# A two-layer ViT tower on one core: the Switch layer's weights made stationary and fetched per tile, its router moved into the hyena tail, its last add made by matmul

## The chip, the cores and the metric

The kernel runs on one core of a Trainium2 chip. TensorE does matmuls into the eight banks of PSUM, VectorE and ScalarE read PSUM and compute elementwise, GpSimd computes elementwise and issues indirect DMAs, SyncE (SP) issues most other DMAs. Every engine runs its own instruction stream; they meet through semaphores. The metric is the time of one execution on the device in microseconds, given as the median of several runs. All data is float32, apart from the operands of the filler matmuls.

## What is computed

Four images of 64x64x3 become 256 tokens each of 192 features, plus one class token: 257 x 4 tokens. Two layers follow. The first has attention and a soft mixture of experts. The second has the hyena operator (a long convolution with gates, an RMS norm and a projection) and a Switch mixture of experts. The change touches the second layer only:

```python
def _L1_attn_ref(inputs, w_in, b_in, w_sf, b_sf, h, norm_w, w_out, b_out):
    # hyena: gates, long convolution, then
    ms = jnp.mean(jnp.square(y), axis=-1, keepdims=True)
    y = y * jax.lax.rsqrt(ms + EPS) * norm_w
    y = jnp.einsum('bld,ed->ble', y, w_out) + b_out
    return y + inputs * SKIP

def _L1_ffn_ref(hidden_states, router_w, wi, wo):     # Switch, 8 experts, 192 -> 768 -> 192
    logits = x @ router_w
    probs = jax.nn.softmax(logits, axis=-1)
    p, e_idx = jnp.max(probs, axis=-1), jnp.argmax(probs, axis=-1)
    # every token goes to one expert, and its result is scaled by p
    h = jax.nn.relu(x @ Wi_e) @ Wo_e
    # returned: the sum over experts of combine * h; each layer is then added to its input
```

## The kernel before

Tokens lie in nine tiles of 128 rows (`NT`): two per image, and one tile `TAIL` with the four class tokens in rows 0, 32, 64 and 96. The residual stream is `k.h` [128, 9, 192]. `build` runs the stages one after another with `run`, which frees the stage's semaphores and puts a barrier of all engines behind each.

**Hyena inputs** (`hyena_inputs`). SP loads weights and constants, the first two band matrices `hy_band` (1540 KB each) and eight spread rows `hy_x_spread`, and as its last act here issues `a["wi"]`, the first-layer weights of all eight Switch experts, 4608 KB, into `k.wi` (L1533).

**Hyena mix** (`hyena_mix`). SP loads five constants, `hy_w_out` (576 KB) among them, into one semaphore `w_in`; TensorE waits for all five before the first convolution. 24 steps m follow, in six groups of four, one band matrix to a group: a row matmul `cls_source` (L1743), a convolution of four matmuls in two column groups (L1755), VectorE's gate (L1846), and a sum matmul `sum_y` (L1765). For each group from the third on SP waits for the convolutions two groups back, loads the band and four `hy_x_spread` rows, and at the end `a["wo"]`, the second-layer weights of all Switch experts. Then `project` (L1802) multiplies by `w_out` with 32-row operands, one row group per image; tile 0 of every image first, tile 1 in two halves because bank 7 (`MS`) still holds the mean squares; VectorE adds into `k.h` (L1857). The class tokens are projected last (L1821).

**Switch** (`stage_switch`). It starts with the layer norm of the nine tiles (`Norm`: `bn_stats` L103, `bn_aggr`, a power on GpSimd L118, subtract and scale L111, transposes L135, copies L145). TensorE makes the router logits with 36 instructions of 8 columns (L2040). VectorE finds the expert of each token; TensorE counts ranks by triangular and ones matmuls (L2048, L2052); VectorE makes from them `dest_rows`, a row of a sorted table in DRAM for each token, and `tile_expert`, the expert of each of its 15 tiles. Every expert's tokens start at a new tile. The table was zeroed by 16 DMAs; nine indirect DMAs on GpSimd scatter the normalised tokens into it (L2019). Between these steps stand filler matmuls (`keep_busy`, L82), queued in TensorE's program order.

The loop runs over 15 tiles, in a ring of three. SP loads a tile of x. TensorE transposes it (L2067, two 96-column halves), ScalarE copies it out (L2124). Layer 1 (L2076): x is stationary, the expert's weights are the moving operand, 2 x 2 matmuls of 384 columns, found by a register read `expert_of`. ScalarE and VectorE apply relu to one half each, TensorE transposes the hidden tile (L2085), both engines copy it out (L2133, L2200), layer 2 (L2094) has six matmuls of 192 columns, VectorE copies (L2205), GpSimd stores to a second table (L2024). TensorE's program order in each turn is: turn x of tile t+1, turn h of t, layer 1 of t+1, layer 2 of t.

After the last store nine indirect gathers fetch the results in token order (L2028), and behind the last of them VectorE does `h += token_y * top_prob` nine times (L2230). A further stage `store` issues eight DMAs to the output.

Of the kernel before, what the change touches and what calls it, by code (L numbers as in the profile page):

```python
# [14 lines left out]
STAGES = 5  # L15

P = 128
# [435 lines left out]


def store(k, out):

    stored = k.sem("out_stored")
    with k.nc.Block() as block:
        @block.sync
        def _(sp):  # L460
            for b in range(B):
                sp.dma_start(out[b, 1:L, :].rearrange("(j p) d -> p j d", p=P),
                             k.h[:, JT * b:JT * (b + 1), :]).then_inc(stored, 16)
                sp.dma_start(out[b, 0:1, :], k.h[QUAD * b:QUAD * b + 1, TAIL, :]).then_inc(stored, 16)
            sp.wait_ge(stored, 16 * 2 * B)

# [1028 lines left out]
def hyena_inputs(k, a, x):  # L1495

    nc, ps = k.nc, k.ps
    with ExitStack() as st:
# [17 lines left out]
        with nc.Block() as block:  # L1516
            @block.sync
            def _(sp):
# [13 lines left out]
                if STAGES >= 5:  # L1532
                    sp.dma_start(k.wi[:, :, :, :], a["wi"]).then_inc(k.s_switch_w, 16)  # L1533
# [123 lines left out]
def hyena_mix(k, a, x):  # L1657
# [6 lines left out]
    with ExitStack() as st:  # L1664
# [26 lines left out]
        with nc.Block() as block:  # L1691
            @block.sync
            def _(sp):
                for dst, n in ((bout[:, :], a["hbout"].broadcast_to([P, D])), (nw[:, :], a["hnw"]),
                               (image[:, :], a["himage"]), (tail[:, :], a["htail"]), (wout[:, :, :], a["hwout"])):
                    sp.dma_start(dst, n).then_inc(w_in, 16)
                for g in range(2, NG):
                    sp.wait_ge(conv, GP_ * (g - 1))
                    x.load_band(sp, a, g)
                    sp.wait_ge(gated, GP_ * (g - 1))  # L1700
                    x.load_x0(sp, g)
                if STAGES >= 5:
                    sp.dma_start(k.wo[:, :, :, :], a["wo"]).then_inc(k.s_switch_w, 16)

            @block.gpsimd
            def _(pool):
# [9 lines left out]

                pool.memset(zero[:, :], 0.0).then_inc(zeroed, 1)
# [16 lines left out]
                pool.tensor_tensor(rms[:, :], mse[:, :], k.half[:, :], ALU.pow).then_inc(rms_r, 1)  # L1734

            @block.tensor
            def _(pe):
# [61 lines left out]
                def project(t, b, c):  # L1799
                    row = slice(QUAD * b, QUAD * (b + 1))  # L1800
                    out = (ps[:, 4 * t + b, 0:D] if (t, b) != (1, 3) else ps[:, MS, 0:D])
                    mm = pe.matmul(out, y[row, c, 1 + t * P:1 + (t + 1) * P], wout[row, c, :],  # L1802
                                   start=c == 0, stop=c == NG - 1)
                    if c == NG - 1 and b % 2 == 1:
                        mm.then_inc(proj, 1)

                pe.wait_ge(gated, PAIRS)
                for c in range(NG):
                    pe.wait_ge(y_r, c + 1)
                    for b in range(B):  # L1810
                        project(0, b, c)
                squares(NG - 1)
                for half in ((0, 1), (2, 3)):
                    if half == (2, 3):
                        pe.wait_ge(mse_r, 2)
                    for c in range(NG):
                        for b in half:
                            project(1, b, c)
                pe.wait_ge(yc_r, NG)
                for c in range(NG):  # L1820
                    mm = pe.matmul(ps[:, MS, D:2 * D], yc[:, c, :], wout[:, c, :], start=c == 0,  # L1821
                                   stop=c == NG - 1)
                mm.then_inc(proj_c, 1)

            @block.scalar
            def _(act):
                act.wait_ge(w_in, 80)
                for c in range(NG):
# [3 lines left out]
                                   ).then_inc(y_r, 1)  # L1832

            @block.vector
            def _(dve):
# [24 lines left out]
                for t in range(JT):  # L1860
                    for b in range(B):
                        if b % 2 == 0:
                            dve.wait_ge(proj, 2 * t + b // 2 + 1)
                        if (t, b) == (1, 3):
                            dve.wait_ge(proj_c, 1)
                            add(TAIL, TAIL, ps[:, MS, D:2 * D])
                            add(JT * b + t, B * t + b, ps[:, MS, 0:D])
                        else:
                            add(JT * b + t, B * t + b, ps[:, 4 * t + b, 0:D])
# [52 lines left out]
HH = HID // 2  # L1922


def alloc_switch(k, a, st):

    k.wi = k.sb("switch_wi", [DK, SE, DC, HID], F32, st)
# [3 lines left out]
    k.sorted_y = k.nc.dram_tensor("sorted_y", ((ST + 1) * P, D), F32, kind="Internal").ap()  # L1931


def stage_switch(k, a):
    nc, ps = k.nc, k.ps
    with ExitStack() as st:
# [3 lines left out]
        rw = sb("router_w", [DK, DC, SE])  # L1940
        tri = sb("before", [P, P])
        desc = sb("descending", [P, NT, SE])
        steps = sb("tile_steps", [P, SE, TOKEN_TILES])
        lower = sb("lower", [P, SE, SE])
        valid = sb("valid", [P, NT])
        spare = sb("spare", [P, NT])
        tile_no = sb("tile_no", [1, ST, SE])
        zeros = sb("zeros", [P, D])
        lm = sb("lm", [P, NT])
        sh = sb("sh", [P, NT, SE])  # L1950
        pe_ = sb("pexp", [P, NT, SE])
        psum_ = sb("prob_sum", [P, NT])
        top = sb("top_prob", [P, NT])
        eq = sb("eq", [P, NT, SE])
        first = sb("first_max", [P, NT])
        oh = sb("one_hot", [P, NT + 1, SE])
# [389 lines left out]
```

## Time and profile before

| | us |
|---|---|
| median of 3 runs | 814.07 |
| lowest and highest | 811.37 and 817.34 |
| the profiled execution | 815.75 |
| its span, first to last instruction | 814.1 |
| mean granted TensorE clock in it | 0.950 |
| TensorE busy | 713.6 (88%) |
| VectorE, ScalarE, GpSimd busy | 287.0, 223.5, 141.5 |

Times in the rows are microseconds from the start of the span. A matmul of float32 appears as two instructions, so "x12" means six matmuls. TensorE's matmuls are listed under PE, its weight loads under PEld, which overlap. The granted clock is given as a share of full speed: 1.00 is 2.4 GHz and 0.50 is 1.2 GHz. In the chain of waits every piece is what the next one waited for.

### The profile page before, as it was taken

To read this page: it belongs to the slowest core of one execution; us is meant where nothing else is said; L and a number is where in the kernel's file an instruction comes from. 1 tells how busy PE (TensorE), PEld (TensorE's weight loads), DVE (VectorE), ACT (ScalarE), POOL (GpSimd) and SP (SyncE) were. 2 spreads that over 40 slices of the span, in tenths; PEclk is the share of its full clock that TensorE was granted. 3 is DMA by queue.
4 is the path that set the end of the run, shared out by engine and by line. 5 is a ranking of instruction groups with operands and counts; after the bars stand their busy time and mean duration, and the time that the engine had idled before them with its cause. 6 is when DMAs were issued, how large, how long until landed. Compare 5 with 4: busy or idle time off the path is not lost. (4 is left out here: it accounts for less than half of the span.)

```text
span 814.1 us, 11798 instructions
## 1 busy us (share of the span) xinstructions
PE 713.6 (88%) x4265; PEld 493.4 (61%) x4266; DVE 287.0 (35%) x618; ACT 223.5 (27%) x486; POOL 141.5 (17%) x194
## 2 busy tenths in 40 slices
PE   4587999999998889899999999989789989699960
PEld 3355854545455444389999998734535655477750
DVE  0003345454552598613233232036312152122211
ACT  2332124333332244244444441014200110122210
POOL 6761201011000053300000000000062113011023
PEclk9998999999999999999999999999679998799995
DMA  8318000000000030038888880035937821111002
GB/s 219 85 8 231 0 2 1 1 1 1 1 2 0 1 78 1 0 98 257 254 261 249 257 249 1 1 122 174 237 91 265 336 88 35 39 39 39 24 24 78
DMA packets 28087, 78.37 MB, mean 96 GB/s; under 512 B 7698, under 2 KB 17934, under 8 KB 26738
## 3 DMA queue, kind: packets, MB, share of 16 engines
q1 hardware_dynamic: 25090, 74.02, 30.7%
q0 software_dynamic: 2960, 3.84, 1.9%
q8 instruction: 26, 0.43, 0.2%
q14 instruction: 11, 0.09, 0.0%
HBM read 72.21 MB, written 5.63 MB: 96 GB/s over the span
## 5 line engine op out<-in xcount | busy, mean ns | idle before, releaser
L1358 PE MATMUL banks<-slots,soft_w 96*128 (+1 forms) x768 | 90.9, 275 | 1.6 <-PEq L1111 1.6
L1358 PEld LDWEIGHTS banks<-slots,soft_w 96*128 96x128 f32 x768 | 89.8, 192 | 1.8 <-issue 1.8
L1418 DVE COPY eo<-banks 32x192 f32 x128 | 45.3, 354 | 106.6 <-PE banks L1369 103.6
L1404 ACT ACTIVATE hid<-banks,soft_b 128x128 f32<-128x128 f32 x192 | 55.5, 368 | 61.4 <-PE banks L1358 61.3
L861 DVE TENSOR_REDUCE nm<-banks 128x2 f32<-128x906 f32 x48 | 53.0, 1103 | 44.2 <-PE banks L661 44.2
L1369 PE MATMUL banks<-soft_w,hid 128*128 128x192 f32 x384 | 67.5, 326 | 0.0
L825 ACT ACTIVATE pt<-banks 128x1024 f32<-128x1024 f32 (+1 forms) x48 | 49.0, 1023 | 58.5 <-PE banks L687 58.5
L1369 PEld LDWEIGHTS banks<-soft_w,hid 128*128 128x128 f32 x384 | 61.7, 190 | 0.0
L661 PE MATMUL banks<-kt,qt 32*128 32x453 f32 x192 | 49.4, 590 | 6.2 <-DVE nm L861 3.8
L82 PE MATMUL banks<-dense 128*128 128x512 bf16 x170 | 44.1, 414 | 11.0 <-PEq L2264 8.7
L687 PE MATMUL banks<-qa,kt 32*128 32x256 f32 (+1 forms) x384 | 51.5, 386 | 0.0
L705 PE MATMUL banks<-pt,vt 128*32 128x257 f32 (+2 forms) x384 | 51.0, 386 | 0.4 <-ACT pt L825 0.3
L2076 PE MATMUL banks<-switch_wi,tile_xt 96*128 x120 | 45.3, 523 | 0.7 <-ACT tile_xt L2124 0.6
L687 PEld LDWEIGHTS banks<-qa,kt 32*128 32x128 f32 (+1 forms) x384 | 32.4, 172 | 12.9 <-issue 9.0
L82 PEld LDWEIGHTS banks<-dense 128*128 128x128 bf16 x170 | 17.1, 105 | 34.0 <-issue 16.2
L1537 POOL MEMSET hy_u<- 96x16 f32 x1 | 0.1, 113 | 201.2 <-POOLq L2264 201.2
L1155 PE MATMUL banks<-phi,xt 96*128 96x512 f32 x72 | 33.8, 618 | 0.0
L705 PEld LDWEIGHTS banks<-pt,vt 128*32 128x32 f32 (+2 forms) x384 | 18.2, 109 | 24.4 <-issue 8.2
L2094 PEld LDWEIGHTS banks<-switch_wo,tile_ht 128*128 128x128 f32 x180 | 30.0, 190 | 4.9 <-issue 1.2
L2094 PE MATMUL banks<-switch_wo,tile_ht 128*128 x180 | 31.8, 326 | 0.9 <-DVE tile_ht L2200 0.9
L2076 PEld LDWEIGHTS banks<-switch_wi,tile_xt 96*128 96x128 f32 x120 | 22.7, 199 | 16.0 <-issue 3.2
L1132 POOL TENSOR_TENSOR cw<-ex,f 128x1024 f32<-128x1024 f32 x9 | 23.2, 2572 | 46.3 <-ACT f L1227 46.3
(267 smaller groups left out, 986.4 us busy)
## 6 DMA issues: line engine op xcount, KB each, us to landing
soft_w<-in_sw SPq DMA_DIRECT2D x64, 576.0 KB, 5.5
hy_band<-in_hband SPq DMA_DIRECT2D x6, 1540.0 KB, 6.6
switch_wi<-in_wi SPq DMA_DIRECT2D x1, 4608.0 KB, 24.9
switch_wo<-in_wo SPq DMA_DIRECT2D x1, 4608.0 KB, 16.3
hy_x_spread<-x_rows SPq DMA_DIRECT2D x24, 128.5 KB, 5.1
vt<-in_vt SPq DMA_DIRECT2D x1, 2496.0 KB
dwc_spread<-dispatch_cls SPq DMA_DIRECT2D x1, 1536.0 KB, 9.0
sorted_x<-zeros SPq DMA_DIRECT2D x16, 96.0 KB, 1.7
```

The costliest lines, as they stand in the source:

```text
L82: pe.matmul(k.ps[:, bank, :], k.dense[:, 0:P], k.dense[:, :], start=True, stop=True)
L661: mm = pe.matmul(ps[:, q, 0:NK], qt[row, c, b, j * P:(j + 1) * P], kt[row, c, b, :], start=True, stop=True)
L687: mm = pe.matmul(ps[0:kr, 2 + s % 2 * 2 + q, u * NP_:(u + 1) * NP_], kt[row, c, b, at:at + kr], qa[row, n % 2, :], start=True, stop=True)
L705: mm = pe.matmul(ps[QUAD * g:QUAD * (g + 1), 6, 0:L], vt[0:vr, tile, at:at + VW], pt[0:vr, s % 4, q, u, :], start=t == 0, stop=t == 3)
L825: act.activation(pt[0:kr, s % 4, :, :, 0:NP_], ps[0:kr, at:at + 2, :].rearrange("p g (t q) -> p g t q", t=2), ACT.Exp).then_inc(exped, 1)
L861: dve.tensor_reduce(nm[:, n % 2, j, at:at + QUAD + 1:QUAD], ps[:, 0:2, 0:NK], AXX, ALU.max, negate=True).then_inc(maxed, 1)
L1358: mm = pe.matmul(ps[:, 2 * (r % 2) + j // 3, (j % 3) * P:(j % 3 + 1) * P], k.w1[r][:, d, j * P:(j + 1) * P], rhs, start=d == 0, stop=d == ...
L1369: mm = pe.matmul(ps[:, 4 + r, 0:D], hid[:, r % 2, j, :], k.w2[r][:, j, :], start=j == 0, stop=j == HJ - 1)
L1404: ins = act.activation(hid[:, r % 2, j, :], ps[:, 2 * (r % 2) + j // 3, (j % 3) * P:(j % 3 + 1) * P], ACT.Gelu, bias=k.b1[:, ds(i * R + r, ...
L1418: dve.tensor_copy(eo[SL * r:SL * (r + 1), b, ds(i, 1), :].rearrange("p e d -> p (e d)"), ps[SL * b:SL * (b + 1), 4 + r, 0:D]).then_inc(eo_ ...
L2076: mm = pe.matmul(ps[:, 1 + c, 0:HH], xst[:, d, :], k.wi[:, ds(e, 1), d, c * HH:(c + 1) * HH].rearrange("p e n -> p (e n)"), start=d == 0, ...
L2094: mm = pe.matmul(ps[:, 5 + r, 0:D], hst[:, j, :], k.wo[:, ds(e, 1), j, :].rearrange("p e n -> p (e n)"), start=j == 0, stop=j == HJ - 1)
```

## The change

It has five parts.

1. `k.wi` and its load in `hyena_inputs` are gone. Each of the 15 tiles loads its expert's first-layer weights, 128 x 1152 floats (576 KB), into a ring of three. SP reads the expert from `tile_expert` into a register and issues the load; it can do so only in the Switch stage.
2. Layer 1 is turned round: the weights are stationary and x moves, 128 columns. K = 192 is split into 128 and 64. The 64-row parts are laid out in the two halves of the partitions, so that even and odd column blocks use different row groups. The product comes out already transposed; `turn_h` and its two copies are gone. The turning of x is one transpose of 128 columns and two matmuls with the identity that write the last 64 features to both halves.
3. Norm, router, zeroing of the tables and scatters move from the Switch stage into the end of the hyena mix (`Route`). The norm is done in two groups, four tiles and five. `project` does tile 1 of all images at once. The zeroing DMAs and router constants are issued by SP near the start of the mix.
4. The router has fewer steps: one comparison fused with a product, the spare rows folded into constants, the totals from a separate small matmul.
5. The last add is made on TensorE: `k.h` by the identity into PSUM, then each gathered tile times a diagonal of `top_prob`, each with a semaphore of its own. ScalarE copies out and SP stores, within the same stage; the stage `store` is gone.

```diff
@@ hyena_inputs, SP
-                if STAGES >= 5:
-                    sp.dma_start(k.wi[:, :, :, :], a["wi"]).then_inc(k.s_switch_w, 16)
@@ hyena_mix, SP, behind the five loads of w_in
+                k.route.load(sp, a)
@@ hyena_mix, GpSimd: first k.route.clear(pool); behind the power of rms:
+                k.route.gpsimd(pool)
@@ hyena_mix, TensorE
+                pe.wait_ge(mse_r, 2)
                 for c in range(NG):
+                    project(1, c)
                 pe.wait_ge(yc_r, NG)
+                pe.wait_ge(h2, 2)
...
                 mm.then_inc(proj_c, 1)
+                k.route.tensor(pe)
@@ hyena_mix, VectorE
+                dve.wait_ge(proj, 1)
+                for b in range(B):
+                    add(JT * b, b, ps[:, b, 0:D])
+                k.route.moments(dve, 0, h2)
+                dve.wait_ge(proj, 2)
+                for b in range(B):
+                    add(JT * b + 1, B + b, ps[:, 4 + b, 0:D])
+                dve.wait_ge(proj_c, 1)
+                add(TAIL, TAIL, ps[:, 1, 0:D])
+                k.route.normalize(dve, 0)
+                k.route.moments(dve, 1, h2)
+                k.route.normalize(dve, 1)
+                k.route.vector(dve)
@@ Route
+    def load(self, sp, a):
+        for dst, n in ((self.rw[:, :, :], "rw"), (self.tri[:, :], "before"), (self.desc[:, :, :], "desc"),
+                       (self.steps[:, :, :], "steps"), (self.lower[:, :, :], "lower"),
+                       (self.tile_no[:, :, :], "tile_no"), (self.place[:, :, :], "place0")):
+            sp.dma_start(dst, a[n]).then_inc(self.c_in, 16)
+        sp.wait_ge(self.zero, 1)
+        for t in range(ST + 1):
+            sp.dma_start(k.sorted_x[t * P:(t + 1) * P, :], self.zeros[:, :]).then_inc(self.cleared, 16)
+        sp.dma_start(k.sorted_y[ST * P:(ST + 1) * P, :], self.zeros[:, :]).then_inc(self.cleared, 16)
+    def tensor(self, pe):
+        keep_busy(k, pe, 0, 8)
+        pe.wait_ge(self.c_in, 112)
+        for n in range(4):
+            turn_x(n)
+        for n in range(4):
+            logits(n)
+        keep_busy(k, pe, 0, 8)
+        for n in range(4, NT):
+            turn_x(n)
+        for n in range(4, NT):
+            logits(n)
+        keep_busy(k, pe, 0, 5)
...
+        mm.then_inc(self.rank, 1)
+        keep_busy(k, pe, 0, ROUTE_FILL)            # ROUTE_FILL = 60
@@ stage_switch, SP
+                def load_wi(i, r):
+                    e = sp.value_load(tei[0:1, ds(i * RING + r, 1)], min_val=0, max_val=SE - 1)
+                    sp.dma_start(wi[r][:, :], a["wi"][ds(e, 1)].rearrange("e p n -> (e p) n")).then_inc(wi_in[r], 16)
+                sp.wait_ge(route.te_r, 1)
+                for r in range(RING):
+                    load_wi(0, r)
+                sp.wait_ge(route.scattered, 16 * NT)
                 for r in range(RING):
                     sp.dma_start(xs[r][:, :], k.sorted_x[r * P:(r + 1) * P, :]).then_inc(xs_in[r], 16)
                 with sp.Fori(1, TURNS) as i:
                     for r in range(RING):
                         sp.wait_ge(xt_m, (i - 1) * RING + r + 1)
                         sp.dma_start(xs[r][:, :], k.sorted_x[ds((i * RING + r) * P, P), :]).then_inc(xs_in[r], 16)
+                        sp.wait_ge(h_m, ((i - 1) * RING + r) * 2 + 2)
+                        load_wi(i, r)
@@ stage_switch, TensorE
                 def turn_x(i, r):
                     pe.wait_ge(xs_in[r], i * 16 + 16)
+                    pe.transpose(ps[:, 0, 0:P], xs[r][:, 0:DA], k.ident[:, :])
+                    for q in range(2):
+                        mm = pe.matmul(ps[q * DB:(q + 1) * DB, 0, P:2 * P], xs[r][:, DA:D], k.ident[:, :],
+                                       start=True, stop=True)
                     mm.then_inc(xt_m, 1)
+                def layer1(i, r, first=False):
+                    pe.wait_ge(wi_in[r], i * 16 + 16)
                     pe.wait_ge(xt_r, i * RING + r + 1)
+                    if not first:
+                        pe.wait_ge(h_a, i * RING + r)
+                        pe.wait_ge(h_v, i * RING + r)
+                    for j in range(HJ):
+                        pe.matmul(ps[:, 1 + j % 2, (j // 2) * P:(j // 2 + 1) * P], wi[r][:, j * P:(j + 1) * P],
+                                  xst[:, 0, :], start=j < 2, stop=False)
+                    for j in range(HJ):
+                        half = slice(j % 2 * DB, (j % 2 + 1) * DB)
+                        mm = pe.matmul(ps[:, 1 + j % 2, (j // 2) * P:(j // 2 + 1) * P],
+                                       wi[r][half, HID + (j // 2) * P:HID + (j // 2 + 1) * P], xst[half, 1, :],
+                                       start=False, stop=j >= HJ - 2)
...
                 with pe.Fori(0, TURNS - 1) as i:
                     for r in range(RING):
                         nxt = (i + (r + 1) // RING, (r + 1) % RING)
                         turn_x(*nxt)
-                        turn_h(i, r)
                         layer1(*nxt)
                         layer2(i, r)
...
+                pe.wait_ge(diag_r, NT)
+                for n in range(NT):
+                    pe.wait_ge(gathered[n], 16)
...
+                    mm = pe.matmul(ps[:, n // 2, at:at + D], diag[:, n, :], yg[:, n, :], start=False, stop=last)
@@ stage_switch, VectorE
-                for t in range(NT):
-                    dve.wait_ge(gathered, 16 * NT)
-                    dve.scalar_tensor_tensor(k.h[:, t, :], yg[:, t, :], top[:, t:t + 1], k.h[:, t, :],
-                                             ALU.mult, ALU.add).then_inc(added, 1)
@@ build
-        run(k, store, out)
```

## Rows read from the trace of the kernel before

**Rows 1.** Chain of waits in the tile loop: start us, us, what.
```profile
698.08 0.65 PE banks L2067 x2
698.75 0.39 ACT tile_xt L2124
...
740.00 2.75 PE banks L2076 x8
742.75 1.95 PE banks L2094 x12
744.70 0.22 PE banks L2067 x2
...
783.68 0.67 PE banks L2085 x6
...
785.28 2.23 PE banks L2094 x12
```

**Rows 2.** Window table: us, busy us (x instructions) per engine, granted clock, DMA share, GB/s.
```profile
600.00:605.00 5.00, 5.00 (x18) 2.44 (x16) 0.85 (x2) 0.00 (x0) 4.92 (x2) 0.50 0.01 3
655.00:659.00 4.00, 2.73 (x20) 2.21 (x16) 2.33 (x7) 0.00 (x0) 0.00 (x0) 1.00 0.00 0
718.00:784.00 66.00, 66.00 (x333) 51.47 (x332) 17.36 (x36) 15.69 (x35) 6.44 (x12) 1.00 0.10 32
```

**Rows 3.** Chain of waits, router and scatters.
```profile
668.62 5.80 PE banks L2040 x36
674.42 3.40 PE banks L82 x8
...
682.30 0.18 DVE dest_rows L2188
...
693.65 2.31 DMA sorted_x<-xn,dest_rows
```

**Rows 4.** Timeline behind the gathers: start us, us, engine, line, what, count.
```profile
803.96 3.05 DVE L2230 SCALAR_TENSOR_TENSOR h<-token_y,top_prob,h 128x192 f32<-128x192 f32 x9 [16.07 <-DMA token_y<-sorted_y,dest_rows]
...
811.68 0.34 SPq L464 DMA_DIRECT2D out<-h  x1
```

**Rows 5.** Timeline, end of hyena inputs and start of the mix.
```profile
570.27 0.59 SPq L1533 DMA_DIRECT2D switch_wi<-in_wi  x1
...
590.64 0.43 SPq L1696 DMA_DIRECT2D hy_w_out<-in_hwout  x1
...
597.27 0.70 PE L1743 MATMUL banks<-hy_row,hy_kv_own 12*128 12x257 f32 x4 [3.45 <-DMA hy_w_out<-in_hwout]
...
606.70 0.70 PE L1743 MATMUL banks<-hy_row,hy_kv_own 12*128 12x257 f32 x4
...
607.33 1.09 PE L1755 MATMUL banks<-hy_band,hy_kv 128*64 128x257 f32 x8
```

**Rows 6.** DMA issues of SP: what, count, KB each, median us to landing.
```profile
hy_band<-in_hband SPq DMA_DIRECT2D x6, 1540.0 KB, 6.6
switch_wi<-in_wi SPq DMA_DIRECT2D x1, 4608.0 KB, 24.9
switch_wo<-in_wo SPq DMA_DIRECT2D x1, 4608.0 KB, 16.3
```

**Rows 7.** Timeline, hyena tail and the norm behind it.
```profile
649.02 2.23 PE L1802 MATMUL banks<-hy_w_out,hy_y 32*128 32x192 f32 x48
...
654.22 2.37 DVE L1857 SCALAR_TENSOR_TENSOR h<-banks,hy_rms,h 128x192 f32<-128x192 f32 x7 [0.75 <-POOL hy_rms L1734]
...
659.52 2.44 DVE L103 BATCH_NORM_STATS2 stats<-h 128x6 f32<-128x192 f32 x9 [1.01 <-PEq L2264]
...
662.86 1.80 POOL L118 TENSOR_TENSOR rs<-veps,half 128x9 f32<-128x9 f32 x1 [3.07 <-DVE veps L108]
...
664.69 2.70 DVE L111 TENSOR_SCALAR xn<-h,mv,rs 128x192 f32<-128x192 f32 x9 [1.91 <-POOL rs L118]
```

**Rows 8.** Timeline, one expert's layer 1 in the soft experts' loop.
```profile
440.31 2.81 PEld L1358 LDWEIGHTS banks<-slots,soft_w 96*128 96x128 f32 x24
```

More of the change, by code:

```diff
@@ L452 @@
 FILL_TOK = 34
[L455 to L465, printed above, removed]
 HEADS = 12
@@ L1858, in add @@
                                              ALU.mult, ALU.add).then_inc(h2, 1)
[L1860 to L1869, printed above, removed]
+                dve.wait_ge(proj, 1)
[3 more added lines that the diff above has]
+                dve.wait_ge(proj, 2)
+                for b in range(B):
+                    add(JT * b + 1, B + b, ps[:, 4 + b, 0:D])
[5 more added lines that the diff above has]
+                k.route.vector(dve)
 def layout_hyena(i):
@@ L1952, in stage_switch @@
[L1952 to L1956, printed above, removed]
-        many = sb("many", [P, SE, TOKEN_TILES])
-        tiles_of = sb("tiles_of", [P, SE])
-        bl = sb("base_terms", [P, SE, SE])
-        base = sb("base", [P, SE])
-        end = sb("end", [P, SE])
-        place = sb("place", [P, NT, SE])
-        dest = sb("dest", [P, NT])
-        desti = sb("dest_rows", [P, NT], I32)
@@ L1992, in stage_switch @@
+        diag_r, summed, final_r, stored = (
+            k.sem(f"switch_{n}") for n in ("top_diag", "summed", "final_ready", "stored"))
         with nc.Block() as block:
@@ L2110, in _ @@
                         turn_x(TURNS - 1, r + 1)
-                    turn_h(TURNS - 1, r)
-                    if r < RING - 1:
                         layer1(TURNS - 1, r + 1)
                     layer2(TURNS - 1, r)
+                pe.wait_ge(xt_r, ST)
+                for g in range((NT + 1) // 2):
+                    t = ORDER_R[2 * g]
+                    rhs = k.h[:, t:t + 3:2, :] if g < NT // 2 else k.h[:, t:t + 1, :]
+                    pe.matmul(ps[:, g, 0:rhs.shape[1] * D].rearrange("p (t d) -> p t d", d=D), k.ident[:, :], rhs,
+                              start=True, stop=False)
@@ L2142, in _ @@
-                ht_copy(ST - 1)
+                    act.activation(hst[:, r, 0, :, :].rearrange("p j q -> p (j q)"), ps[:, 1, 0:HP * P],
+                                   ACT.Relu).then_inc(h_a, 1)
+                act.wait_ge(route.top_r, 1)
+                for n in range(NT):
+                    act.activation(diag[:, n, :], k.ident[:, :], ACT.Copy, scale=route.top[:, n:n + 1]
+                                   ).then_inc(diag_r, 1)
+                with act.Fori(0, TURNS) as i:
+                    for r in range(RING):
+                        tile(i, r)
```

474 lines of the change are left out of this document (258 added, 216 removed).

## The prediction

> **What bounds the kernel now.** I read the chain of waits first. From the end of the hyena stage it is one strand. The tile loop of the Switch stage takes 698.08 to 787.50, and in it TensorE is the limit. The chain runs over nothing else there, tile after tile: 2.75 us of layer 1, 1.95 of layer 2, 0.22 for turning x and about 0.66 for turning the hidden tile, together 5.57 us a tile [rows 1]. The window table has TensorE busy for all 66 us from 718 to 784, at a granted clock of 1.00, which is the 2.4 GHz level [rows 2]. Ahead of the loop the strand is serial: VectorE, GpSimd and small matmuls up to `dest_rows` at 682.48, then the indirect scatters, whose last lands at 695.96 [rows 3]. Behind it come nine gathers, nine adds, a stage change and eight stores, issued one by one, the last at 811.68 [rows 4]. Further forward, the timeline shows the convolution waiting for data: `hy_w_out` is issued at 590.64 and the first convolution matmul starts only at 597.27, idle until then for that load (3.5 us), with the 4608 KB of `switch_wi` issued on the same queue at 570.27 and landing 24.9 us later, at 595.2 [rows 5, 6].
>
> The sum has five terms, A to E, each from one stretch. A positive term is time saved.
>
> **A, the start of the mix.** `switch_wi` is no longer loaded ahead. On SP's queue a 1540 KB load lands after 6.6 us and a 4608 KB one after 16.3 [rows 6]: 9.7 us for 3.14 MB, 3.1 us per MB, and some 1.7 us of latency left over. `hy_w_out`, 576 KB, then lands 3.5 us after its issue, at 594.2, and the wait falls by 3.0. The constants, two memsets and 17 zeroing DMAs of the router now stand in this stage, behind `hy_w_out` on SP: 24 issues of about 0.46 us end near 602.3, while the next band is due for issue at about 600.7. It lands 6.6 later, at 608.9, just when its group of matmuls begins; I take 0 for it, 1 at most. The clock comes on top. It is at 0.50 from 600 to 605 [rows 2], after the 3.5 us of idling, and the first group took 9.4 us (597.27 to 606.70) where the same work at the full clock is about 6.4: two pairs of row matmuls at 0.63 (606.70 to 607.33), four convolutions and one pair of sums at about 1.02 (a convolution's 1.09, less what overlaps the next) [rows 5]. With 0.5 us of idling left I expect the clock to stay up: 3.0 more. A = +6.0; bounds 0 (the load is late for another reason) and 6.2.
>
> **B, hyena tail and router, up to `dest_rows`.** The anchor is the first projection matmul, 649.02 [rows 7]. Before, from there to 682.48: 33.5 us. After, step by step. Five of six projection groups 1.8, squares 0.8, mean 0.2, then GpSimd's power 1.8 with 0.2 of handing over: 653.8. Four adds at 0.34 (2.37 for seven): 655.2. Four `bn_stats` at 0.27 and their aggregates 0.5: 656.8. Five more adds: 658.5. Four normalised tiles at 0.30: 659.9. Five statistics: 661.8; second power 1.9: 663.7; five tiles 1.5: 665.3 [rows 7]. TensorE keeps up: four row groups at once do 48 instructions in 2.23 us [rows 7], and the TAIL projection, eight fills, the first transposes and half of the logits lie in VectorE's time. After the last tile come its transposes and copy, 0.6, and ten logit matmuls, 20 instructions. The trace has 36 in 5.80 us over a fall of the clock [rows 3]; I take 2.8: 668.7. From logits to `dest_rows` the old way is 8.1 us (674.42 to 682.48), of which TensorE's eight fills at the low clock held 3.40 [rows 3]. The new way is bounded by 4.9 (clock high: five VectorE steps, the total, 16 rank instructions, four steps of 0.26) and 6.7 (low: five fills 2.1, rank 3.0). I take 5.6: 674.3. B = +8.2; bounds 5.9 and 9.7.
>
> **C, from `dest_rows` to the first tile.** Before 15.6 us (682.48 to 698.08). The scatters cost the same 12.1 of GpSimd's issue (682.48 to about 694.6, the last one's start at 693.65 and about one more [rows 3]), to 686.4. The 60 fills queued on TensorE need 60 x 0.214 = 12.8 (half of the 0.43 that eight took at the low clock [rows 3]) from about 673.4, so they just end with them; every microsecond at the low clock delays the stage change by half. Then the stage change, a new piece here: VectorE sat 1.01 us in the one before [rows 7]. Only behind it does SP issue three loads of 576 KB, each after reading the tile's expert into a register, and only then the first x tile, on the same queue. The three loads are 1.77 MB, 5.5 us at the rate above. A register read shows nowhere by itself; TensorE makes two per tile without losing time in 5.57 us, so it costs 0 to 2.8; I take 1.0, since the loop shows no trace of them. The x tile then lands 1.4 + 1.7 + 5.5 + 0.3 = 8.9 after the change, 696.3, instead of 2.1 us after the last scatter [rows 1, 3]. ScalarE's nine copies for `diag` are hidden in it. C = 22.0 instead of 15.6 = -6.4; bounds -11 (reads of 2.8) and -2 (x not queued behind the weights).
>
> **D, the loop.** Gone per tile: six transposes and their wait, 0.66 + 0.02. Layer 1, before 8 instructions of 384 columns, is now 12 of K=128 and 12 of K=64, each of 128 columns. The nearest row is the soft experts' layer 1, weights stationary, 128 columns: 24 weight loads in 2.81 us, 0.114 between starts [rows 8]. So the first 12 cost 1.37. If the K=64 halves did not overlap they would cost the same again and layer 1 would be 2.74, as now. Row groups do overlap here: four of them give 0.046 per instruction of 192 columns [rows 7] against 0.163 in layer 2 (1.95 for 12) [rows 1]. Two groups should give 3 x 0.22 = 0.66. The convolution, which goes over to column groups and back, takes 1.09 for two pairs of 257 columns [rows 5], where 2 x 2 x 257 columns at layer 2's rate are 0.87: about 0.15 per change of shape. Layer 1 gets two: 1.37 + 0.66 + 0.3 = 2.35. The turning of x is one transpose, a change and four column-group instructions, about 0.65 to the end of the last. And it is now followed at once by layer 1 of the same tile, where the hidden transposes stood between them before: ScalarE's copy, 0.39, and 0.2 around it are no longer covered [rows 1]. Turn and copy together 1.23. Period 1.23 + 2.35 + 1.95 = 5.53, against 5.57: next to nothing. Bounds 5.2 (free changes) and 6.2 (halves in series). The expert's weights, 3.6 us from issue, come three slots ahead of use, over 10 us: hidden. At the ends something is won: the last tile's hidden transposes and copies (783.68 to 785.28 [rows 1]) go, 1.6, and the first tile, at half clock, loses its own. First tile 6.2, 14 periods 77.4, 0.5 for the rest of the low clock, last layer 2 2.25: 86.35 instead of 89.45. D = +3.1; bounds -6.5 and +7.7.
>
> The Trainium skill speaks against this part: "TensorEngine Tiling (Array Packing)", Key Properties, says that a change of the tiling mode, not of the tile, drains the engine, and the kernel now makes four a tile. The trace's 0.15 agrees in kind. With four visible changes instead of three the period would be 5.68 and the total 2 us later.
>
> **E, the end.** Gathers, unchanged, land at 803.94, just before the first add. Before, from there to 814.1: 10.2 us: adds 3.05, stage change 1.0, eight issues, of which the last starts at 811.68, and 2.4 to the end [rows 4]. After: one matmul pair at half clock 0.8, a copy 0.35, one issue of the TAIL rows, 2.4, and 0.1 of waits: 3.7. The other eight tiles are added and stored while gathers still come in. E = +6.5; bounds 5.5 and 7.
>
> **Sum.** 6.0 + 8.2 - 6.4 + 3.1 + 6.5 = 17.4. The profiled execution took 815.75 (span 814.1), 1.7 above the median 814.07, so it would give 798.4, and the median 796.7.
>
> **Rivals.**
> - *The halves run in series, or each change of shape costs 0.3.* Period 6.2: 14 x 0.7 = 9.8 more, 806.5. Against it: the 0.046 of the row groups. For it: no row shows K=64, and the change is made twice per layer. 0.14.
> - *The mix does not start earlier* (its constants or their own latency bind). A = 0: 802.7. For it: many small loads stand in that queue. 0.10.
> - *The x tile is not queued behind the weights, and changes of shape are free.* C = -3 and D = +6: 790.4. Against it: `hy_band` and what is issued behind it. 0.15.
> - *Slower: TensorE's clock falls in the loop.* Every tile now has a gap of about 0.6 us. At the 1.2 GHz level all but the copy doubles, 4.8 us per tile, 67 us in all: some 864. It decides from two tiles at the low level onward for every further one; 1% slower is reached with about five. Against it: from 655 to 659 TensorE was busy for only 2.73 of 4 us, at clock 1.00 [rows 2]; the loop will have 88%. The Trainium skill, "TensorE: Matmul & The Clock Gate", adds that transposes do not count as activity in the same way; a tile has one. 0.05.
>
> **How the numbers follow.** The forecast case has 0.56, with its own range 790 to 804 from the bounds of B, C and E. The range of 8 in 10, 789 to 807, takes in the first three rivals. A measurement can tell about 1% here: 805.9 is the line. Faster by over 1%: 0.56 + 0.10 + 0.15, less a little for several bounds at their bad end, 0.79. Within 1%: the first rival and that remainder, 0.15. Slower: 0.06.
>
> **What would show it.** Convolution starting near 594.2 with clock 1.00 after it (A); `dest_rows` 25 us behind the first projection (B); 22 us from there to the first tile, its x landing last (C); 5.5 us between tiles, with TensorE idle about 0.6 before layer 1 (D); under 4 us from the last gather to the end (E). A period above 6 or a first tile more than 26 us behind `dest_rows` would make the prediction wrong.

## The result, and the profile after

The changed kernel takes 805.14 us (median of 4, 803.93 to 805.52) against 814.5 for the old one timed beside it: a ratio of 0.9883, 95% interval 0.9845 to 0.9922. It is 1.2% faster. The forecast was 796.7, range 789 to 807: direction and wide range held, but the gain is little over half of the 17.4 us forecast, and 805.14 lies just outside the forecast case's own range of 790 to 804. Ratios here and below leave out executions more than 1.5% above the fastest of the same kernel. The profiled execution took 805.52, span 803.8, so by span the gain is 814.1 - 803.8 = 10.3. A stretch "to `dest_rows`" ends where that instruction ends.

| stretch | before | after | gained | forecast |
|---|---|---|---|---|
| up to the issue of `hy_w_out` | 590.64 | 591.12 | -0.5 | 0 |
| A, from there to the first projection | 58.38 | 53.19 | +5.2 | +6.0 |
| B, to `dest_rows` | 33.46 | 27.07 | +6.4 | +8.2 |
| C, to the first tile | 15.60 | 24.05 | -8.4 | -6.4 |
| D, tile loop | 89.42 | 87.3 | +2.1 | +3.1 |
| to the last gather's landing | 16.44 | 16.93 | -0.5 | 0 |
| E, from there to the end | 10.16 | 4.12 | +6.0 | +6.5 |

The timeline after, for the start of the mix (start us, us, engine, line, what, count, idle before and its releaser), answers to [rows 5]:

```profile
590.03 1.84 DVE L1823 TENSOR_TENSOR hy_kv_own<-hy_own_pair,hy_kv_cls 128x768 f32<-128x768 f32 x1 [6.08 <-POOL hy_kv_cls L1703]
591.12 0.51 SPq L1680 DMA_DIRECT2D hy_w_out<-in_hwout  x1
...
595.74 0.70 PE L1729 MATMUL banks<-hy_row,hy_kv_own 12*128 12x257 f32 x4 [1.43 <-DMA hy_w_out<-in_hwout]
...
601.99 0.70 PE L1729 MATMUL banks<-hy_row,hy_kv_own 12*128 12x257 f32 x4
```

TensorE's wait for `hy_w_out` is 1.43 us where it was 3.45, and the first group takes 6.25 us (595.74 to 601.99) where it took 9.4. The window table (columns as in [rows 2]) shows why, and shows the clock further on:

```profile
600.00:605.00 5.00, 5.00 (x32) 2.75 (x34) 1.28 (x3) 0.13 (x1) 5.00 (x3) 1.00 0.57 171
...
656.00:660.00 4.00, 4.00 (x21) 2.39 (x21) 2.23 (x12) 0.00 (x0) 1.17 (x1) 0.71 0.00 0
660.00:666.00 6.00, 5.90 (x36) 4.40 (x36) 1.44 (x7) 2.90 (x5) 0.00 (x0) 0.78 0.00 0
666.00:672.00 6.00, 6.00 (x26) 4.86 (x26) 2.69 (x14) 0.00 (x0) 0.00 (x0) 0.50 0.02 3
...
704.00:770.00 66.00, 60.07 (x486) 51.78 (x485) 10.99 (x24) 10.10 (x23) 6.04 (x11) 1.00 0.44 139
```

From 600 to 605 the clock is at 1.00 where it was 0.50, and 32 matmul instructions are done instead of 18. In the router, 656 to 672, it is at 0.50 to 0.78, although TensorE is busy nearly throughout. In the tile loop it stays at 1.00 with 6 of 66 us idle.

From the scatters to the first tile, the timeline after:

```profile
666.73 3.56 PE L2122 MATMUL banks<-route_one_hot,ones 128*128 128x64 f32 x16
...
670.15 15.37 PE L82 MATMUL banks<-dense 128*128 128x512 bf16 x59
...
671.21 0.17 DVE L2061 CAST route_dest_rows<-route_dest 128x9 int32<-128x9 f32 x1
...
682.55 0.96 POOL L2079 DMA_INDIRECT sorted_x<-xn,route_dest_rows  x1 [0.30 <-issue]
686.49 1.86 ACT L2287 ACTIVATE top_diag<-ident,route_top_prob 128x128 f32<-128x128 f32 x6 [21.30 <-PEq L2356]
687.47 0.36 SPq L2170 DMA_DIRECT2D tile_wi<-in_wi  x1
```

The last scatter starts at 682.55, the fills end at 685.52 (670.15 + 15.37), and the stage change lets ScalarE start at 686.49. The chain of waits (start us, us, what) continues from there, where before it went from the last scatter's landing to the x tile at once:

```profile
688.63 0.34 SPq L2170
...
689.02 0.27 SPq L2169
...
689.73 0.34 SPq L2170
...
690.11 5.18 DMA route_tile_x<-sorted_x
...
695.43 0.45 PE banks L2210
```

SP's issues of the expert weights are 1.1 us apart (688.63 to 689.73), one register read (L2169) and one issue (L2170) each. Only then is x issued (690.11), and it lands 5.18 later. The chain in the loop, one tile and a piece, answers to [rows 1]:

```profile
707.66 0.11 PE banks L2210
707.76 0.39 PE banks L2212 x4
708.16 0.02 issue
708.18 0.39 ACT tile_xt L2279
708.57 0.04 issue
708.62 1.60 PE banks L2223 x12
710.22 0.87 PE banks L2227 x12
711.09 2.15 PE banks L2238 x12
713.24 0.11 PE banks L2210
```

Turn of x 0.50, an uncovered copy and its hand-overs 0.45, layer 1 2.47, layer 2 2.15: 5.58. Every third tile, once per pass of the hardware loop, the issue piece ahead of L2223 is some 0.2 longer. The mean over the 12 tiles behind the low clock (707.49 to 775.03) is 5.63. The end, by the chain, answers to [rows 4]:

```profile
796.74 2.94 DMA token_y<-sorted_y,route_dest_rows
...
799.72 1.02 PE banks L2270 x2
...
800.76 0.33 ACT final L2295
```

### The profile page after: what moved, and what is told of

Read it like the earlier page. It is cut to its first block and busy times, and to the rows that moved or that the text cites. A ratio compares the mean times of both kernels' runs of the same rounds, so it can differ in the third digit from the quotient of the medians.

```text
span 803.8 us, 12174 instructions
## 1 busy us (share of the span) xinstructions
PE 713.8 (89%) x4482; PEld 500.8 (62%) x4492; DVE 275.3 (34%) x593; ACT 221.2 (28%) x485; POOL 141.9 (18%) x195
## 3 DMA queue, kind: packets, MB, share of 16 engines
HBM read 76.37 MB, written 5.63 MB: 102 GB/s over the span
## 5 line engine op out<-in xcount | busy, mean ns | idle before, releaser
L2302 DVE TENSOR_SCALAR tile_ht<-banks 128x384 f32<-128x384 f32 x15 | 8.4, 558 | 74.0 <-PE banks L2227 74.0
L2223 PE MATMUL banks<-tile_xt,tile_wi 128*128 128x128 f32 x180 | 25.2, 292 | 8.2 <-ACT tile_xt L2279 7.2
L647 PEld LDWEIGHTS banks<-kt,qt 32*128 32x128 f32 x192 | 14.4, 183 | 26.7 <-DVE nm L847 21.2
```

The source lines that it names most:

```text
L647: mm = pe.matmul(ps[:, q, 0:NK], qt[row, c, b, j * P:(j + 1) * P], kt[row, c, b, :], start=True, stop=True)
L2223: pe.matmul(ps[:, 1 + j % 2, (j // 2) * P:(j // 2 + 1) * P], wi[r][:, j * P:(j + 1) * P], xst[:, 0, :], start=j < 2, stop=False)
```

## Experiments

Three theories went to the chip. A: the start of the mix gains because the 4608 KB load is no longer in the way of `hy_w_out`. C: the first tile waits for x behind three weight loads, and those could be issued before the stage change; the fills delay that change. D: the layout as such is quicker, and what keeps the period at 5.6 is the uncovered copy. The rivals: constants and latency bind A; contention or the weights' own landing binds C; changes of the array's shape, or the K=64 part, bind D.

The time ahead of the hyena stage differs between the groups of runs (the old kernel took 812.6 beside the first four, 850.9, in one execution, beside the next four, 834.0 beside the last four) and between executions of one group. So ratios are compared where there are several rounds, and stretches inside the profiles elsewhere; a stretch is one execution's.

**The changed kernel itself, again.** No edit.

> The changed kernel again, unedited, as the yardstick of the runs beside it: ratio to the kernel before 0.988 (about 9.4 us less), period of the tile loop 5.58 to 5.6 us, nine microseconds from the stage change to the first tile.

Measured: 803.28 (802.45 to 805.75), ratio 0.989, interval 0.9841 to 0.9938. The stretches repeat: first projection 640.35, `dest_rows` 667.25, last scatter 678.44, stage open 682.50, first tile 691.9, first gather 783.03.

**Fewer fills behind the rank.**

```diff
-    ROUTE_FILL = 60
+    ROUTE_FILL = 45
```

> Fillers behind the ranks cut from 60 to 45. Theory (the fillers, run at the low clock for their first 5 us, end 2.0 us after the last scatter is issued, and so hold the stage change): they now end before it, the stage change comes 2.0 us earlier and the whole kernel is 2.0 us shorter than the changed one. Rival (they keep TensorE's clock up for the loop): the first tiles get slower and nothing is gained, -0.5 to +3 us.

Measured: 803.39, ratio 0.9895 (0.9837 to 0.9952). The expected 2.0 us did not come: the fills cost nothing that counts. Its timeline gives the reason:

```profile
675.75 0.38 PE L82 MATMUL banks<-dense 128*128 128x512 bf16 x1
...
678.67 0.96 POOL L2079 DMA_INDIRECT sorted_x<-xn,route_dest_rows  x1 [0.30 <-issue]
682.37 1.86 ACT L2287 ACTIVATE top_diag<-ident,route_top_prob 128x128 f32<-128x128 f32 x6 [19.03 <-PEq L2356]
```

The fills are done by 676.1, yet the stage opens only at 682.37, 3.70 after the last scatter's start. In eight further kernels this distance is 3.67 to 3.69. Where the fills end later, they bind instead: in the changed kernel they end at 685.52 and the stage opens 0.97 after them, in its repeat at 681.52 and 0.98 after. So the opening is the later of "last scatter + 3.69" and "fills + 0.98"; the fills cost 0.25 us in the changed kernel and 0.4 in its repeat.

The same profile held a second finding. Up to the rank the two programs are the same, but here the clock did not fall (window table, columns as before; first the kernel with 45 fills, then the changed kernel's repeat):

```profile
646.00:676.00 30.00, 28.70 (x215) 19.19 (x214) 14.72 (x65) 4.07 (x7) 9.91 (x9) 1.00 0.05 18
```

```profile
653.00:663.00 10.00, 9.93 (x53) 6.85 (x54) 3.56 (x14) 2.91 (x5) 1.02 (x1) 0.71 0.00 0
663.00:673.00 10.00, 10.00 (x38) 5.72 (x38) 2.34 (x12) 0.00 (x0) 3.93 (x4) 0.60 0.09 31
```

From the first projection to `dest_rows` it took 23.4 us at 1.00 throughout, against 26.9 in the repeat and 27.1 in the changed kernel, so the fall costs 3.5 to 3.7 us. TensorE's instructions in this stretch are the same in twelve kernels: it took 23.3 to 23.4 in two of them and 24.3 to 27.5 in the ten others, so whether, when and for how long the clock falls differs from one execution to the next. The two without a fall are the two with 45 fills. Those fills come only behind the stretch, and the mean clock of this kernel's four executions (0.949 to 0.958) is no higher than the repeat's (0.951 to 0.959); with one profile of each kernel, that their number matters is neither shown nor excluded. What this execution won in the router it lost half of in the loop: first tile to first gather took 92.85 us against 91.1, with the second tile's layer 1 still at the low clock. TensorE had been idle for 15.3 us before the first tile instead of 10.4. So the recorded rival, that the fills shorten the slow start of the loop, is not excluded.

**GpSimd waits for its scatters before it leaves the stage.**

```diff
                                     k.xn[:, n, :], None).then_inc(self.scattered, 16)
+        pool.wait_ge(self.scattered, 16 * NT)
```

> GpSimd waits for its nine scatters to land at the end of the hyena stage, before the stage change. Theory (the stage's end waits for the landing of GpSimd's own DMAs anyway): the next stage opens 3.7 to 4.0 us after the start of the last scatter, as without the wait. Rival (GpSimd only needs a fixed time to leave the stage): the landing, 2.3 us after the start, and then the fixed 2.7 us, 5.0 us in all.

Measured: last scatter 702.68, stage open 706.94, 4.26 later. The rival's 5.0 is out: a wait for the landing put on top of what GpSimd does anyway costs at most 0.6, and the fills, which ended at 705.87 here, account for nearly all of that (0.98 behind them is 706.85). So GpSimd leaves the stage about when its scatters have landed (2.3 us from start, by the DMA issues) plus 1.4, with or without the wait. That the landing is what it waits for fits, but isn't separated from work of its own of the same length.

**The first three experts' weights issued before the stage change.** Rings and load moved into the router's object; SP issues them at the end of the hyena stage.

```diff
                 sp.dma_start(k.wo[:, :, :, :], a["wo"]).then_inc(k.s_switch_w, 16)
+                k.route.prefetch(sp, a)
...
-                sp.wait_ge(route.te_r, 1)
-                for r in range(RING):
-                    load_wi(0, r)
```

> The first three expert weights are issued by SP at the end of the hyena stage, as soon as the tile experts are known, under the scatters, and no longer behind the stage change. Theory (the first x tile is queued behind 1.77 MB of weights): from the stage change to the first transposing 2.5 us instead of 9.0, 6.5 us less in all, and up to 3 more if TensorE's clock survives the shorter gap. Rival (the x tile is late for another reason, such as the latency of the scatters): under 2 us less.

Measured: 798.53 (796.81 to 799.98), ratio 0.9827 (0.978 to 0.9874). Its chain of waits and timeline at the opening:

```profile
683.30 1.29 SPq L2186 DMA_DIRECT2D route_tile_x<-sorted_x  x3
...
685.40 0.44 PE L2219 MATMUL banks<-ident,route_tile_x 128*128 128x128 f32 x1 [3.23 <-DMA route_tile_x<-sorted_x]
```

The x tile is used 2.06 us after the opening (683.34) instead of 8.94: 6.9 us of C came from issuing the three weight loads behind the stage change and ahead of x. The rival of under 2 us is out. Queue order and the loads' contention with x went together here; x issued first, with the weights behind it, was not tried. The medians differ by 4.75 and the first gathers by 6.6 (776.42 against 783.03); why the medians differ by less is not shown.

**x turned one tile further ahead.**

```diff
                 with pe.Fori(0, TURNS - 1) as i:
                     for r in range(RING):
-                        nxt = (i + (r + 1) // RING, (r + 1) % RING)
-                        turn_x(*nxt)
-                        layer1(*nxt)
+                        layer1(i + (r + 1) // RING, (r + 1) % RING)
+                        turn_x(i + (r + 2) // RING, (r + 2) % RING)
                         layer2(i, r)
```

> In the tile loop x of tile t+2 is turned between layer 1 of t+1 and layer 2 of t, so that ScalarE's copy lies under layer 2. Theory (the copy, 0.39, and its hand-overs stand uncovered before every layer 1): the wait of about 0.6 per tile goes, one more change of array shape (0.2) is seen; period 5.2 instead of 5.6, 5 to 6 us less in all. Rival (the period is set by something else, such as the weights' arrival): no change.

Measured: 794.64 (791.8 to 796.25), ratio 0.9762 (0.9712 to 0.9812). The chain in its loop:

```profile
704.59 0.26 PE banks L2210
704.85 0.37 PE banks L2212 x4
705.21 2.15 PE banks L2238 x12
707.36 1.34 PE banks L2223 x12
708.70 0.87 PE banks L2227 x12
```

The period is 4.98 (704.59 to 709.57), with no piece of ScalarE in it. That is better than the 5.2 expected. Against 5.58 the copy and its hand-overs are gone (0.45) and L2223 takes 1.34 instead of 1.60; the turn takes 0.13 more. L2223 now follows layer 2 at once, and its first weight load lies under it, where before it stood behind a wait and behind the turn's column groups; which of the two the 0.26 belongs to isn't separated. First tile to first gather is 82.6 instead of 91.1: 8.5 us, four times what D gained.

**Layer 1's K=64 part left out** (the last 64 of the 192 inputs don't reach layer 1).

> Layer 1 leaves out its twelve K=64 instructions, so features 128 to 191 do not enter; everything else stays. Theory (each change of the array's shape costs about 0.2): the 0.87 go, and layer 2 falls from 2.15 to 1.95, so the period is 4.5 us instead of 5.6. Rival (layer 2's 2.15 has another cause, changes of shape are free): 4.7 us with layer 2 at 2.15.

Measured: period 4.52. L2223 stays at 1.60, and layer 2 is 1.95 again, as in [rows 1]:

```profile
740.06 1.60 PE banks L2223 x12
741.67 1.95 PE banks L2233 x12
```

So the K=64 part costs 0.87 of its own and 0.20 in the instructions behind it; together that is the difference of the periods, 1.06. Going back from row groups to the full array costs 0.20 us, and the rival of free changes (4.7) is out. With x turned ahead, layer 2 followed column groups instead, and took 2.15 there too.

**All twelve K=64 instructions in one half of the rows** (the odd ones then read the wrong half's weights).

```diff
-                        half = slice(j % 2 * DB, (j % 2 + 1) * DB)
+                        half = slice(0, DB)
```

> All K=64 matmuls of layer 1 read the lower half of the partitions, so that odd column blocks get the wrong 64 rows of weights; the number of instructions is the same. Theory (even and odd halves run side by side in two row groups): in one row group they run in series, 0.87 becomes 1.5 to 1.6, period 6.2 to 6.3 us. Rival (they never overlapped): 5.6 us as it is.

**The second part with all 128 rows instead of 64** (twelve full instructions in place of the split ones, on data that isn't the layer's).

```diff
-                        half = slice(j % 2 * DB, (j % 2 + 1) * DB)
+                        half = slice(0, P)
```

> The second part of layer 1 uses all 128 partitions, so that even and odd blocks' weights are both multiplied in and the product is wrong; twelve instructions as before, but no change of shape between layer 1 and layer 2. Theory (0.2 per change, halves overlap): 1.37 for the second part and 1.95 for layer 2, period 5.9 us against 5.6. Rival (what the two row groups gain is lost in changes of shape): 5.6.

Measured, each kernel's chain, first one half, then all rows:

```profile
743.55 1.60 PE banks L2223 x12
745.15 1.53 PE banks L2227 x12
```

```profile
742.16 1.58 PE banks L2223 x12
743.74 1.34 PE banks L2227 x12
745.08 1.95 PE banks L2238 x12
```

In one half L2227 takes 1.53, and the period is 6.24 us, as expected; in two halves 0.87. The two row groups do work side by side, and that is worth 0.66 a tile: the rival of halves in series falls. With all rows the period is 5.86, near the 5.9 expected. They take 1.34, with no change of shape behind, so 3.29 with layer 2 against 3.02 split: what the split wins over plain instructions is 0.27 a tile, 4 us over the 15 tiles.

**A 4608 KB load back in its old place.** First the load of `wo` moved there, which has 128 partitions; then, in a run of its own, the old first-layer weights in their 96-partition layout as an array that nothing reads.

```diff
                     x.load_x0(sp, g)
+                sp.dma_start(k.wi96[:, :, :, :], a["wi96"]).then_inc(k.s_switch_w, 16)
```

> The 4608 KB of second-layer weights are issued at the end of the hyena inputs, where the first-layer weights used to be, and no longer behind the last band. Theory (the early start of the convolution comes from the empty queue): from the mix stage's start to the first projection 60.2 us as in the kernel before, instead of 55.0, with the clock at 0.50 in the first group. Rival (the start is earlier for another reason, or the clock's fall has another cause): 55 us.

> The 4608 KB of first-layer weights are loaded again where they used to be, in their old layout of 96 partitions, beside everything the change does; nothing reads them. Theory (this transfer, still under way, held back hy_w_out): its landing takes some 24 us as before instead of the 14.1 of the 128-partition load put there, from VectorE's first own-pair product to the first convolution matmul 8.0 us instead of 5.3 to 5.7, and to the first projection 59.8 instead of 54.3, with the clock at 0.50 in the first group. Rival (something else in the change made the start earlier): 5.7 and 54.3.

From the own-pair product's start on VectorE (589.25 before, 590.03 after) to the first convolution matmul, and to the first projection:

| kernel | to the convolution | to the projection | `hy_w_out` lands in |
|---|---|---|---|
| before | 8.0 | 59.8 | 6.6 |
| after | 5.7 | 54.3 | 4.6 |
| `wo` there | 5.3 | 53.9 | 4.2 |
| 96-partition load there | 7.9 | 59.6 | 6.7 |

The DMA issues of the second (what, count, KB each, median us to landing) and its timeline, which answer to [rows 5, 6]:

```profile
switch_wi<-in_wi SPq DMA_DIRECT2D x1, 4608.0 KB, 24.9
switch_wo<-in_wo SPq DMA_DIRECT2D x1, 4608.0 KB, 16.1
hy_w_out<-in_hwout SPq DMA_DIRECT2D x1, 576.0 KB, 6.7
```

```profile
615.31 0.70 PE L1730 MATMUL banks<-hy_row,hy_kv_own 12*128 12x257 f32 x4 [3.59 <-DMA hy_w_out<-in_hwout]
```

With the 96-partition load the old wait (3.59 against 3.45), the old landing and the low clock behind it (0.50 from 618 to 623) are back: 5.3 us, which is theory A. With `wo` nothing is back, for it had landed: 14.1 us after its issue, before `hy_w_out` was issued. The expectation for `wo`, 60.2, failed for that reason. What stood in the way was not 4608 KB on the queue but a load of this size that takes 24.9 us. The constant `hy_b_out` (96 KB), issued 1.8 us ahead of `hy_w_out`, tells the same: it landed in 6.0 us in the old kernel and 6.3 with the 96-partition load, and in 2.6 in the other two. The Trainium skill, "DMA: Bandwidth & Descriptors", Rules for kernel authors, puts the most bandwidth at 128 partitions; the rows agree, 24.9 us with 96 partitions against 14.1 to 16.5 with 128. The two layouts also differ in bytes per partition (48 and 36 KB), so the count of partitions alone isn't shown as the cause.

**All that helped, together**: 45 fills, the early weights, x a tile ahead, and `hy_w_out` as the first of its five loads instead of the last; then the same with two of the first fills moved in between the logits.

```diff
-                for dst, n in ((bout[:, :], a["hbout"].broadcast_to([P, D])), (nw[:, :], a["hnw"]),
-                               (image[:, :], a["himage"]), (tail[:, :], a["htail"]), (wout[:, :, :], a["hwout"])):
+                for dst, n in ((wout[:, :, :], a["hwout"]), (bout[:, :], a["hbout"].broadcast_to([P, D])),
+                               (nw[:, :], a["hnw"]), (image[:, :], a["himage"]), (tail[:, :], a["htail"])):
```

> Early weights, x turned a tile ahead, 45 fillers, and hy_w_out issued first of its five: the sum of what each gave alone in its own stretch. 6.9 at the loop's start, 8.6 in the loop, 0.3 at the stage change and 1.2 at the mix's start: 17 us less than the changed kernel, ratio to the kernel before 0.967. Rival (x turned ahead needs the weights sooner than they come, or the gains overlap): 12 us or less.

> The combination, with the eight fillers between the two halves of the logits spread: two inside the first half, and one each behind two of the later transposings. Theory (the tail stands just at the edge at which the clock falls, and dense work put earlier keeps it up): clock 1.00 from the first projection to dest_rows, 23.2 us for it instead of 26.9, 3 us less than the combination. Rival (the fall does not depend on where these few stand): the same to 0.5 us more.

Measured: the first has a ratio of 0.9675 (0.9624 to 0.9726), the second 0.9685 (0.9638 to 0.9733). Both beat the old kernel, by 3.2%, and by their ratios the changed one, which was not timed beside them, by a further 2%. The single gains (6.9 for the weights, 8.5 for x, 1.2 for `hy_w_out`: own-pair product to convolution 4.5 instead of 5.7) sum to 16.6, and (0.9883 - 0.9675) x 814.5 is 16.9. The 1.2 was not run by itself; in the nine kernels that leave that order alone the stretch took 5.2 to 5.8, so it is 0.7 to 1.3. The chain of the first kernel at its opening:

```profile
716.73 1.84 DMA route_tile_x<-sorted_x
...
718.70 0.45 PE banks L2219
```

It opens 3.67 after its last scatter (713.09 to 716.76), uses x 1.9 later, and needs 82.0 from there to its first gather. Its profiled execution took 819.91, with the first projection only at 678.56; the extra time lies ahead of these stretches. Moving the fills changed nothing that can be told: in the first kernel the clock stayed at 1.00 through the router (first projection to `dest_rows` 23.3), in the second it fell near 700 (25.3), the reverse of what the moved fills were to do. One profile of each isn't enough to say that they harm; what decides the fall stays open.

## Why the forecast was right, and where it was too high

Every sign held, and the mechanism of every term but for one step of C; the sizes were all too hopeful. The terms came out 7.1 us short in sum: C 2.0, B 1.8, D 1.0, A 0.8, E 0.5, and half a microsecond each ahead of the mix and in the gathers, which the forecast took as unchanged. In C and D the sums came closer than their parts, by luck.

**A, right in cause, 0.8 short.** "`hy_w_out` then lands 3.5 us after its issue" was worked out from size alone; it landed in 4.6, and 1.43 us of waiting stayed. The clock's part, 3.0, was right (first group 6.25 against 9.4). That the load in its way was one of 24.9 us in 96 partitions, and that its size alone would not have been in the way, the forecast didn't see; it made no difference here, since the load went altogether. The band behind the 17 zeroing DMAs cost nothing, as taken: from the second group to the first projection it is 42.3 us before and after.

**B, 1.8 short.** The step that failed is "I take 5.6" for the way from the logits to `dest_rows`. Up to the end of the logits (664.35) it was 20.0 us from the first projection, 19.7 by the steps. From there it was 7.0: the 16 rank instructions took 3.56 (bound at the low clock 3.0) and four fills 1.81. The clock stood at 0.50 to 0.78, so this is past the low-clock bound of 6.7. The kernel with 45 fills showed the other case: 18.4 to the end of the logits and 5.0 behind it, 23.4 us in all, a gain of 10.1, above the upper bound of 9.7. So nearly half of what the clock decides lies ahead of the logits' end. The forecast took a middle where single executions lie anywhere between the two cases, 23.3 to 27.5.

**C, 2.0 short, by one term.** The stage change was put at 1.0 behind the scatters' issue, from VectorE's 1.01 in [rows 7]; it comes 3.69 after the last scatter's start, where the forecast had 1.9 (682.55 to 684.5): 1.8 us. This is the step that failed. In [rows 3] the scatter's landing, 2.31, was already on the path, but the forecast let the stage change run beside it instead of behind it. The fills added 0.25. The second step, 8.9 from the change to the first x tile, measured 8.9 by luck. SP took 3.6 for reads and issues until x was issued, where 1.4 was put; from there to the landing it took 5.2, where 1.7 + 5.5 + 0.3 = 7.5 was put. Two errors of 2.2 cancel; the first weights were issued at 687.47, and so under way while SP read for the next. The rival "x isn't queued behind the weights" is refuted; the early weights show what that would be worth, 6.9.

**D, 1.0 short.** Mean period 5.63 against 5.53: 1.4 over 14 tiles, of which the ends gave back 0.4. Within the period of 5.58, turn, copy and hand-overs took 0.95 against 1.23, layer 1 with its changes of shape 2.47 against 2.35, and layer 2 2.15 against 1.95, since a change of shape stands in front of it too. That these cancel to 0.05 is luck. In layer 1 the K=128 part was 1.60 instead of 1.37 (1.34 where it follows layer 2 directly), and the K=64 part 0.87. The forecast's 0.15 per change of shape was itself misread: 1.09 less 0.87 is 0.22 for two changes, 0.11 each, and the one that the runs isolate took 0.20. The other 0.05 of the mean is the loop's own, every third tile. The rule of the Trainium skill that spoke against this part ("TensorEngine Tiling (Array Packing)", Key Properties: a change of mode drains the engine) holds in kind: 0.20 in front of layer 2 goes when the row groups go. What the changes at the turn cost was not isolated. Of the two periods in the forecast, 5.53 with three visible changes and 5.68 with four, the mean of 5.63 lies nearer to the second. The rival of halves in series, which put the period at 6.2, is refuted: 6.24 with all of them in one half, 5.58 as the kernel has it. That the period hardly changes, because the copy comes out from under its cover, was right.

**The slower rival** (clock falls in the loop, 864) is refuted: 60.07 of 66 us busy, at 1.00.

**E** was 0.5 short: the last pair took 1.02 against 0.8, and from the output's issue to the end it was 2.7 (801.12 to 803.8) against 2.4.

## What to carry to other kernels

A swap of the stationary and the moving operand saves transposes, but put on the clock what those transposes covered: here the copy behind them came out and ate the gain until x was turned a tile further ahead (8.5 us of 803). What a stage needs first must be first in its queue, and what doesn't depend on a barrier belongs before it: three weight loads issued behind a stage change and ahead of x cost 6.9 us, which the same loads in front of it gave back. When a stage ends with indirect DMAs, price its end from the last one's landing, not from its issue.

## What the runs showed of the chip

- A stage whose last work is an indirect scatter opens the next one 3.67 to 3.70 us after that scatter's start, in nine kernels; where TensorE's fills ended last, 0.97 to 0.98 after them, in three.
- A 4608 KB load took 24.9 us with 96 partitions, twice, and 14.1 to 16.5 us with 128.
- SP needs 1.1 to 1.2 us for one register read and the DMA that uses it.
- Two row groups of 64 took 0.87 us for 12 instructions that took 1.53 in one and 1.34 with all 128 rows; going back to the full array cost 0.20.
- The same instructions ran at clock 1.00 in two executions (23.3 and 23.4 us) and slower in ten (24.3 to 27.5); in one of these the clock was 0.71 and 0.60, with TensorE busy for 9.9 and 10.0 of 10 us. The Trainium skill, "TensorE: Matmul & The Clock Gate", Part 1: The HAM clock gate, says that the judging of activity runs freely and doesn't start with the kernel. By that, equal instructions could be judged differently from one execution to the next; it would fit, and no run here tests it.
